# Every second first key of the edge-maximum passes moves from GpSimd to VectorE

## What is computed

```python
def _sage_pool_layer(x, src, dst, Wp, bp, Ws, Wn, b, n_nodes):
    m = jax.nn.relu(x @ Wp + bp)
    msgs = m[src]
    agg = jax.ops.segment_max(msgs, dst, num_segments=n_nodes)
    agg = jnp.where(jnp.isfinite(agg), agg, 0.0)
    return x @ Ws + agg @ Wn + b
...
h = _sage_pool_layer(x, src, dst, Wp1, bp1, Ws1, Wn1, b1, n)
h = jax.nn.relu(h)
h = _l2norm(h)
h = _sage_pool_layer(h, src, dst, Wp2, bp2, Ws2, Wn2, b2, n)
```

## Time and profile before

| | us |
|---|---|
| median of three runs | 2772.53 |
| their range | 2771.99 to 2778.91 |
| the profiled execution | 2772.04 |
| its span in the trace | 2770.3 |
| first edge-maximum pass, in the trace | 662.2 to 1168.6 |
| second edge-maximum pass, in the trace | 1229.7 to 1740.2 |

### The profile page before, as it was taken

How to read it: one execution, slowest core, us unless ns; L and a number is a source line. 1 busy time by engine, 2 the same in 40 slices (tenths; PEclk the granted TensorE clock), 3 DMA queues, 4 the chain that set the end, 5 groups by cost and what they waited for, 6 DMA issues and landing times. The chain is left out here.

```text
span 2770.3 us, 72947 instructions
## 1 busy us (share of the span) xinstructions
PE 2500.8 (90%) x29568; PEld 2013.3 (73%) x29568; DVE 1823.9 (66%) x5033; ACT 1158.4 (42%) x2585; POOL 1280.8 (46%) x1575
## 2 busy tenths in 40 slices
PE   6998999996899999678999996479899999999999
PEld 3666777764666666446666665469899999999998
DVE  6997999987889888448889885310444444444444
ACT  5997888874444444324444444210411111111110
POOL 4007999983888888558888887310000000000000
PEclk8558999997999999689999997579999999999999
DMA  5103000004555555535555556369000000000000
GB/s 167 42 2 103 12 13 12 12 20 125 135 135 142 141 127 147 129 92 129 138 138 136 138 132 166 107 222 345 33 2 2 2 2 2 2 2 1 2 2 19
DMA packets 147301, 226.91 MB, mean 82 GB/s; under 512 B 55184, under 2 KB 113259, under 8 KB 146290
## 3 DMA queue, kind: packets, MB, share of 16 engines
q1 hardware_dynamic: 121502, 185.74, 22.4%
q0 software_dynamic: 21920, 35.15, 6.4%
q10 hardware_dynamic: 3540, 1.30, 0.2%
HBM read 121.74 MB, written 100.35 MB: 80 GB/s over the span
## 5 line engine op out<-in xcount | busy, mean ns | idle before, releaser
L1892 POOL DMA_INDIRECT max_row<-table,max_src_rows x608 | 656.2, 1079 | 173.3 <-issue 154.2
L1934 PE MATMUL max_far<-adj 128*96 128x512 f16 x2200 | 599.9, 386 | 8.0 <-DVE adj L2060 4.1
L2060 DVE TENSOR_SCALAR adj<-adj,node_numbers 128x512 f16<-128x512 f16 x1100 | 391.3, 376 | 122.6 <-PE max_far L1934 89.1
L1758 POOL TENSOR_SCALAR e<-e 128x512 f32<-128x512 f32 (+1 forms) x625 | 365.7, 604 | 178.4 <-ACT e L1746 160.8
L2405 PE MATMUL prop<-g,adj 128*128 128x192 f16 x4608 | 386.4, 247 | 9.4 <-DVE g L2479 9.4
L1772 DVE TENSOR_TENSOR e<-e,a_ps 128x1024 f32<-128x1024 f32 (+1 forms) x313 | 372.1, 1194 | 32.6 <-PE a_ps L1684 12.6
L2405 PEld LDWEIGHTS prop<-g,adj 128*128 128x128 f16 x4608 | 379.9, 98 | 14.1 <-issue 9.2
L2405 PE MATMUL prop<-weights_then_states,adj 128*128 128x192 f16 x4608 | 384.3, 246 | 0.0
L2405 PEld LDWEIGHTS prop<-weights_then_states,adj 128*128 128x128 f16 x4608 | 378.9, 98 | 3.7 <-issue 2.5
L1746 ACT ACTIVATE e<-s_ps 128x512 f32<-128x512 f32 (+1 forms) x625 | 335.4, 585 | 60.0 <-PE o_ps L1696 38.6
L1934 PEld LDWEIGHTS max_far<-adj 128*96 128x96 f16 x2200 | 255.6, 129 | 127.5 <-issue 14.9
(11 more groups left out here) (292 smaller groups left out, 3613.5 us busy)
## 6 DMA issues: line engine op xcount, KB each, us to landing
weights_then_states<-weights SPq DMA_DIRECT2D x100, 400.0 KB, 5.0
weights<-max_rows_w SPq DMA_DIRECT2D x52, 400.0 KB
rows_dram<-max_out SPq DMA_DIRECT2D x100, 192.0 KB
weights<-adj SPq DMA_DIRECT2D x48, 400.0 KB
max_same<-same_dram SPq DMA_DIRECT2D x196, 96.0 KB
rows_dram<-adj SPq DMA_DIRECT2D x96, 192.0 KB
max_row<-table,max_src_rows POOLq DMA_INDIRECT x608
adj<-ids_dram SPq DMA_DIRECT2D x44, 128.0 KB
```

What stands on the lines that cost most here:

```text
L1758: nc.gpsimd.tensor_scalar(e_tile(u), e_tile(u), math.exp(10.0), math.exp(-10.0), ALU.min, ALU.max).then_inc(clipped, 1)
L1892: nc.gpsimd.indirect_dma_start(row[i % RING][:, j, :], None, table_dram, bass.IndirectOffsetOnAxis(ap=src_rows[:, 4 * n + j:4 * n + j + 1] ...
L1934: mm = nc.tensor.matmul(far_ps[j % 2][0:D, :], parts[:, k, a, :], hot[(T * j + k) % HOTS], start=k == a == 0, stop=k == T - 1 and a == 1)
L2060: nc.vector.tensor_scalar(hot[i % HOTS], ids[j % 2], numbers[:, k:k + 1], None, ALU.is_equal).then_inc(hot_made, 1)
```

## The change

Of the first keys of a pass GpSimd keeps those of the steps 4, 6, 8, ... 98, which are 48. The other 52, those of steps 0 to 3 and then of the odd steps, are made by VectorE in `keys_of`, as window 0 of `key_hot`, ahead of the step's other keys. GpSimd numbers its own keys by their place in the list `firsts`, in the same ring of four buffers, so one buffer comes round after eight steps. TensorE waits for `first_key_made` where GpSimd made the key and for `hots_ready`, counted anew, where VectorE did. What is computed is the same.

```diff
--- before.py
+++ after.py
@@ -1826,6 +1826,8 @@
         key_hot = [sb(f"key_hot{i}", [P, WIDEST, FEW_KEYS + 3], F16) for i in range(2)]
         first_key_hot = [sb(f"first_key_hot{i}", [P, FEW_KEYS + 3], F16) for i in range(FIRSTS)]
         first_key_made = sem("first_key_made")
+        firsts = [k for k in range(PARTS) if k >= AHEAD and (k - AHEAD) % 2 == 1]
+        firsts_until = lambda n: sum(k < n for k in firsts)
         keys, lanes, weights = pass_tables(tables)
         columns = key_order(adj)
         behind_out = more[:, T * P + 2 * 8 * D:2 * NP - P]
@@ -1879,10 +1881,11 @@
         @block.gpsimd
         def _(pool):
             def first_key(k):
-                if k >= FIRSTS:
-
-                    pool.wait_ge(hots_used, k - FIRSTS + 1)
-                nc.gpsimd.tensor_scalar(first_key_hot[k % FIRSTS][:, 0:FEW_KEYS], columns, keys[:, first_win[k]:first_win[k] + 1], None, ALU.is_equal).then_inc(first_key_made, 1)
+                i = firsts_until(k)
+                if i >= FIRSTS:
+
+                    pool.wait_ge(hots_used, firsts[i - FIRSTS] + 1)
+                nc.gpsimd.tensor_scalar(first_key_hot[i % FIRSTS][:, 0:FEW_KEYS], columns, keys[:, first_win[k]:first_win[k] + 1], None, ALU.is_equal).then_inc(first_key_made, 1)
 
             def gather(n, j):
                 i = nth[n]
@@ -1893,8 +1896,9 @@
                                              bass.IndirectOffsetOnAxis(ap=src_rows[:, 4 * n + j:4 * n + j + 1], axis=0)
                                              ).then_inc(gathered[j], 16)
 
-            for k in range(AHEAD):
-                first_key(k)
+            for k in firsts:
+                if k < AHEAD:
+                    first_key(k)
             for n in range(PARTS):
                 if n in nth:
                     if nth[n] >= RING:
@@ -1902,7 +1906,7 @@
                         pool.wait_ge(turned, nth[n] - RING + 1)
                     gather(n, 0)
                     gather(n, 1)
-                if n + AHEAD < PARTS:
+                if n + AHEAD in firsts:
                     first_key(n + AHEAD)
                 if n in nth:
                     gather(n, 2)
@@ -1942,12 +1946,13 @@
                 pe.wait_ge(lanes_ready, n + 1)
                 for w in range(STEP_WINS[n % QUARTER]):
                     m = window_dst(WIN_AT[n % QUARTER] + w)
-                    hot_of = key_hot[n % 2][:, w, 0:FEW_KEYS] if w else first_key_hot[n % FIRSTS][:, 0:FEW_KEYS]
+                    by_pool = w == 0 and n in firsts
+                    hot_of = first_key_hot[firsts_until(n) % FIRSTS][:, 0:FEW_KEYS] if by_pool else key_hot[n % 2][:, w, 0:FEW_KEYS]
                     keys_of = hot_of.rearrange("p (k d) -> p k d", k=T)[:, :, 0:m]
-                    if w == 0:
-                        pe.wait_ge(first_key_made, n + 1)
+                    if by_pool:
+                        pe.wait_ge(first_key_made, firsts_until(n) + 1)
                     else:
-                        pe.wait_ge(hots_ready, first_win[n] - n + w)
+                        pe.wait_ge(hots_ready, first_win[n] + w + 1 - firsts_until(n + 1))
                     for h in range(2):
                         mm = nc.tensor.matmul(by_source(n)[:, :, FEW * w:FEW * w + m], lanes_by_weight(n)[:, h, w, :], keys_of,
                                               start=w == 0 and h == 0, stop=h == 1, skip_group_check=True)
@@ -2016,7 +2021,7 @@
             def keys_of(n):
                 first, m = first_win[n], STEP_WINS[n % QUARTER]
 
-                for w in range(1, m):
+                for w in range(int(n in firsts), m):
                     nc.vector.tensor_scalar(key_hot[n % 2][:, w, 0:FEW_KEYS], columns, keys[:, first + w:first + w + 1], None, ALU.is_equal).then_inc(hots_ready, 1)
 
             def weigh(n):
```

## The result

| | before | after |
|---|---|---|
| median, us | 2775.72 | 2737.68 |
| range, runs | 2771.99 to 2785.74, 4 | 2732.32 to 2744.68, 4 |
| profiled execution (span) | 2772.04 (2770.3) | 2741.78 (2740.0) |
| first pass, in the trace | 662.2 to 1168.6 | 662.6 to 1152.2 |
| second pass, in the trace | 1230.1 to 1740.2 | 1214.1 to 1704.6 |

The ratio is 0.9868, 95% interval 0.9844 to 0.9892: 38 us less in the medians, and the forecast was 2734. A pass is counted from its first instruction on VectorE, which in the second pass of the kernel before stands at 1230.1 us and not at 1229.7. The passes together went from 1016.5 to 980.1 us in the profiled executions.

The account below looks back on a forecast made before the run. GpSimd sets the pace, 19.9 us for four steps, with TensorE close behind at 19.2 to 19.3. Gains of 24 (middles), 6.8 (starts) and 9 (ends), less 2 for VectorE, take 37.8 us from 2772.04: 2734, range 2706 to 2758.

Parts of the forecast that it names:

- the 37.8 of the sum: Whole kernel: total gain forecast in us, 39.8 from less waiting of TensorE less 2 for VectorE's added keys.
- GpSimd gets ahead until its ring of four row buffers is full, and then waits for TensorE: Both passes: GpSimd falls to 18.4 us for four steps, below TensorE's 19.2 to 19.3; further savings become waits.
- That part is not GpSimd's and stays: Middles: of 38 us lost in the first, only 12.9 are gathers; the rest, such as ScalarE's 22.6 us "remote", remains.
- The middles: Middle stretch of each pass, steps 8 to 88: TensorE's 28.1 us of gather waits go but a seventh, gaining 24.
- The starts: Start of each pass, ring empty: fewer keys ahead of the first gathers save 3.4 us a pass, 6.8 together.
- The ends: End of each pass: a full ring brings the second near the first, 8 us, plus 1 for the first.
- 2 us expected: VectorE's 104 added keys: mostly hidden under its idle time and lead, costing 2 us; 18 to 28 if all exposed.
- three signs of being wrong: TensorE's lay-out waits for VectorE's keys beyond 5 us, mean gathers above 1.15 us, or unlabelled stalls going too.
- signs of being right: Among them: less "issue" idle, middles' row waits under 8 us, four steps 19.2, VectorE's waits below 42.2, second end 43 to 50.
- Rival 1: Passes: all GpSimd's relief arrives, four steps fall from 19.9 to 18.4 us, 73 us less, 2699; chance 0.15.
- Rival 2: Passes: VectorE's added keys hold GpSimd up, giving back 18 to 28 us; gain 20 us, 2752; chance 0.15.
- Rival 3: Passes: no change, as row waits are about a transfer's landing or late keys cancel the gain; 2765 to 2772; chance 0.10.

Follow-up runs that it names:

- e1: The kernel before, unchanged, profiled once more for a second trace: 2778.57 us in 1 run.
- e2: The changed kernel with two sets of gather semaphores, so a gather waits for the landing eight gathers back, not four: 2685.87 us, ratio 0.9686.
- e5: The changed kernel with all first keys on VectorE and two sets of gather semaphores: 2653.15 us, ratio 0.9555 to the kernel before.
- e3: The changed kernel with all 200 first keys of both passes on VectorE: 2673.75 us, ratio 0.9627 to the kernel before.
- e9: e2 without VectorE's 104 added keys, TensorE reading the key of window 1 instead (wrong weights): 2680.37 us, ratio 0.9661 to the kernel before.
- e4: The kernel before, GpSimd making all first keys and VectorE also making 104 that nobody reads: 2777.12 us, ratio 1.0006.
- e10: The changed kernel with the store of each weight-matrix tile two rounds later: 2699.70 us, ratio 0.9728 to the kernel before.
- e8: The changed kernel with GpSimd making the keys of odd steps 3 to 99, VectorE the others: 2724.81 us, ratio 0.9802 to the kernel before.

## Why the prediction was right, and where it was not

In short: GpSimd set the pace of the passes before the change and still sets it after. Its work and waits became 38.5 us shorter over both passes, and the time fell by about as much; the prediction had TensorE take over the pace.

**The time, 2734 against 2738: right, but two terms were wrong in opposite ways.** GpSimd needed 656.2 + 173.3 + 160.8 + 6.2 = 996.5 us before, 998.5 in e1, and 619.3 + (288.1 - 54.2) + 103.6 + 3.2 = 960.0 us after, 19.2 us for four steps and not 18.4. Without landing waits it went from 998.5 - 27.3 = 971 to 878 us: 93 us less, where the prediction had 104 x 0.70 = 73 (e2 has 79 by the same count: 655.6 + 225.5 - 54.1 - 11.4 + 73.2 + 3.0 = 892). Of the 93 us the keys give 67 (167.6 + 6.4 less 103.6 + 3.2), about their price, and shorter gathers 28 (647.0 in e1, 619.3 after), for which nothing was forecast. Against that stand 54 us of landing waits more. What is left, 998.5 - 960.0 = 38.5 us, is near the 37.8 of the sum by luck. The step that failed is "GpSimd gets ahead until its ring of four row buffers is full, and then waits for TensorE": it waits for its own gathers instead, 81.6 us, and never for TensorE. The wait that the prediction showed for this, 1.12 us at 1140.10, was a "remote" one; e1, with its records whole, has no wait of GpSimd for TensorE in either pass.

**TensorE's other stalls.** "That part is not GpSimd's and stays" was wrong. e1 shows that these rows came from lost records, and e5, with middles at 18.08 and 18.11 us for four steps, that all 38 to 40 us over the floor in a middle of e1 came from GpSimd. The 19.2 us for four steps of the prediction is 19.9 less gather waits that the trace had undercounted; the 19.24 of the changed kernel is GpSimd's new pace. That the two agree is an accident. In e1 26.5 us of gather waits stand beside 40 us over the floor, after 15.8 us beside 24: about 1.5 us lost for one that is shown as a wait for GpSimd.

**The middles:** 24 us expected, 16.3 + 13.8 = 30 against e1, 35 against the first trace (402.9 and 401.7 us). Of 28.1 us of waits 4 were to stay; in fact 32 us stand there, but 54 us had been there before by e1, and the time lost around them was left out.

**The starts:** 6.8 us expected, 0.8 + 3.2 = 4.0 against e1. TensorE's wait for gathers in the first start is 3.2 us, hardly less than the 3.9 of the earlier trace rows. With no key on GpSimd at all (e3) it is 1.2 us, and the starts are 4.4 and 5.3 us shorter than in e1. So the term was an upper end; what eats the rest in the changed kernel was not tried.

**The ends:** 9 us expected, 1.3 + 4.3 = 5.6 against e1, and 1.5 us longer against the first trace, where the end was shorter. This term had a misread row under it. In the earlier trace rows the turn at 1125.48 is that of block 90; block 89 was turned at 1117.38. So the first pass needed 51.2 us, not 43.1, and the passes differed by 4, not by 12.3. After the change the timeline of the second pass has, for the turn of block 89 and the last copy:

```profile
1651.03 0.61 PE L1927 MATMUL max_col<-ident,max_row 128*96 128x128 f16 x8
...
1704.13 0.49 ACT L2117 ACTIVATE max_out<-max_back 128x384 f32<-128x384 f32 x1 [1.07 <-PE max_back L1983]
```

53.6 us, outside the 43 to 50 that were given. In e5, where the ring does fill, it is 38.2. TensorE's clock differs there too, which the prediction left out: over the two ends the granted clock is 0.70 and 0.69 in e1, 0.77 and 0.69 in the changed kernel, 0.86 and 0.83 in e5, against 1.00 in the changed kernel's middles, so a part of the ends runs at 1.2 GHz and not at 2.4. TensorE's busy time in both ends, 107.0 us in e1, 105.3 after and 90.4 in e5, holds what this costs: up to 1.7 of the 5.6 us, and up to 17 of the 40 between e1 and e5.

The three parts make 40 us against e1, and e1's execution is 36.8 us longer: outside the passes the profiled changed kernel took 3.0 us more, in code that the change does not touch. The profiled execution of the changed kernel is also 4 us above its median. Sizes below some 4 us can't be read from single traces here.

**VectorE:** 2 us expected, about 5.5 measured (e9 against e2), nothing measurable while GpSimd holds the pace (e4). The 18 to 28 us of its rivals did not come. VectorE waits 45.1 us for TensorE in the middle, not below 42.2; but e1 has 50.6, and e2, e3 and e5 have 21 to 23. TensorE waits 13.5 us for keys of VectorE, over the bound of 5 that was given, but in two waits, of 7.2 and 6.3 us at the first step of each pass; in e1 two waits of 7.0 and 6.0 us stand there for VectorE's lanes. No later step waits for such a key. So of the prediction's three signs of being wrong this one came only in form, and "if the unlabelled stalls go too" came in full, if only because the records were whole; mean gathers stayed below 1.15 us. Of its signs of being right, "issue" idle hardly fell (154.2 to 152.3 us), and TensorE's waits for rows in the middles were 22.2 us and not under 8.

**The rivals.** Rival 1, all of GpSimd's relief arrives, had the right mechanism: the passes do follow GpSimd, and the other stalls are late effects of its gathers. It was wrong on its landing waits. With these removed, in e2, the time is even below its 2699. Rival 2, that added keys hold GpSimd up, priced at 18 to 28 us: e4 and e9 put it at 0 and about 5.5 us. The Trainium skill's page "SBUF — State Buffer", section "Who interferes with whom", would have a VectorE tensor_scalar in a two-port mode shut GpSimd out for its length. The first keys did get longer, 1079 ns in the mean against 804, but 763 ns in e2 with the same keys on VectorE: the number of keys that VectorE makes does not lengthen them. What does was not tried. Rival 3's "landing of a transfer" was there, as a wait of GpSimd and not of TensorE.

**What delays the landing.** That the gathers land late behind the store, and that this goes for the most part when the store moves, is shown (e10). Why is shown in part. The first data packet of the gather of 884.58 moves at 888.40, 3.8 us after its issue; those of the gathers of 881.99 and 883.32 moved after 1.7 us. Over all 45 late gathers the median is 3.7 us, over the gathers away from the stores 1.7. Of the queues only SyncE's moves anything from 885.6 to 888.3 us, at a share of 1.02 of the 16 engines:

```profile
q1 hardware_dynamic: 115, 0.63, 102.4%
```

So about 2 of the 3 us that a late landing takes longer than the median are gone before its data start to move, behind the store's. The Trainium skill's page "DMA: Bandwidth & Descriptors", section "Queues, rings and completion order", says that an engine takes packets of its queues by turns, and that a transfer's semaphore is raised only after every earlier write of that DMA engine, in other queues too. By the second part alone the data could be there in time and only be reported late; the trace has the data themselves late. Whether it also holds back the report, in the last 1 us, no run here separates from slower data. Of turns the trace shows none for the gathers' queue in these 2.7 us.

## What to carry to other kernels

Taking work from a queue also takes away the time that hid its waits: before removing an instruction, ask of each wait behind it how late its signal is in the worst round, not in the median one (here 6.0 against 3.0 us). Let such a wait reach one buffer further back; here that took four semaphores more a pass and was worth 52 us, more than the change itself. And where a trace shows waits for "remote" or long "issue" on engines that should be fed, take a second trace before any of it is counted as another cause, and check which block a row belongs to by counting from the pass's start.

## What the runs showed of the hardware that was not expected

- A gather issued within 1 us behind a store of 2 x 400 KB from another queue landed about 6 us after its issue in most cases, against 3.0 us in the median; its data began to move after 3.7 us instead of 1.7.
- GpSimd's rounds stay in step with the store's period of four rounds (41 of the 45 long waits end 6.8 to 7.6 us after a store): the landing waits changed from 81.6 us to 27.2 with the parity of the steps whose key was kept (e8), and to 27.8 with the round of the store (e10), 13 and 38 us of time.
- The same GpSimd key, 128 x 125, took 704 ns in the median before, 1046 after, and 672 in e2.
- Two traces of the same kernel held 24,634 and 38,006 semaphore records, and the lack showed only as "remote" waits and as waits that were missing or too short.
